# A selective-state kernel: TensorE's third state product moved behind exp(A) and the first two differences

## The reference

```python
proj = einsum('bsd,ed->bse', x, in_proj_w)            # gate, x/B/C, dt
hBC  = silu(causal_conv4(x/B/C) + conv_b)             # depthwise, 4 taps
L    = exp(segsum(dt * A))                            # decay inside a chunk
Y_diag = einsum('bzlhn,bzshn,bhzls,bzshp->bzlhp', C, B, L, x * dt)
states = einsum('bzlhn,bhzl,bzlhp->bzhpn', B, decay_states, x * dt)
prev   = states carried on from chunk to chunk with exp(A_last)
Y_off  = einsum('bzlhn,bzhpn,bhzl->bzlhp', C, prev, exp(A_cum))
y = (Y_diag + Y_off + x * D) * silu(gate)
out = einsum('bsi,oi->bso', rmsnorm_by_group(y) * norm_w, out_proj_w)
```

## Time and profile before

| what | value |
|---|---|
| median of 3 executions | 1913.36 us |
| profiled execution | 1919.0 us |
| its span | 1917.2 us |
| PE busy with matmuls | 1828.7 us, 95% |
| DVE busy | 1294.0 us, 67% |
| ACT busy | 1061.2 us, 55% |
| POOL busy | 938.7 us, 49% |
| mean granted TensorE clock | 0.983 of full speed |

### The profile page before, as it was taken

One profiled execution on the slowest core, in us unless ns is written; L12 is line 12 of the kernel. 1 busy time (PEld: TensorE's weight loads), 2 busy tenths in 40 slices (PEclk: granted clock), 3 DMA queues, 4 the chain that ended last, 5 costly groups with the idle time before them and its releaser, 6 DMA issues.

```text
span 1917.2 us, 31312 instructions
## 1 busy us (share of the span) xinstructions
PE 1828.7 (95%) x9752; PEld 1408.7 (73%) x9752; DVE 1294.0 (67%) x2094; ACT 1061.2 (55%) x1935; POOL 938.7 (49%) x717
## 2 busy tenths in 40 slices
PE   7889999999999999999999999999999999999966
PEld 6767778777777777777777777777777777777745
DVE  4856667666766667666676667666676666766688
ACT  5455555656546565555546565465665555565632
POOL 1225464555435465354645554354654545454564
PEclk9799999999999999999999999999999999999988
DMA  4412121121212121021211112121211212112121
GB/s 173 142 51 70 53 64 48 39 61 52 70 33 64 48 67 50 28 67 58 66 44 45 57 49 70 33 64 48 67 50 30 65 59 64 43 46 61 34 94 55
DMA packets 76393, 114.14 MB, mean 60 GB/s; under 512 B 21696, under 2 KB 27328, under 8 KB 75328
## 3 DMA queue, kind: packets, MB, share of 16 engines
q1 hardware_dynamic: 58656, 80.07, 14.2%
q10 hardware_dynamic: 17568, 31.99, 5.0%
HBM read 88.94 MB, written 23.07 MB: 58 GB/s over the span
## 4 chain that ended last, share of the span: by engine, by line
issue 45%; POOL 33%; PE 12%; DVE 4%; ACT 2%; DMA 1%; SPq 1%; POOLq 1%; ACTq 0%; DVEq 0%
POOL yt L1505 9%; POOL ssq L1500 6%; POOL wg_lo L1436 4%; POOL wo_lo L1436 4%; POOL prev L1486 3%; POOL yt L1508 3%; POOL wx_lo L1436 3%; PE bank L449 3%; PE bank L451 2%; PE bank L450 2%; PE bank L586 1%; PE bank L479 1%; PE bank L734 1%; PE bank L648 1%; PE bank L782 0%
## 5 line engine op out<-in xcount | busy, mean ns | idle before, releaser
L1505 POOL TENSOR_TENSOR yt<-yt,ea 128x384 f32<-128x384 f32 (+1 forms) x128 | 189.9, 1483 | 413.2 <-DVE ea L1352 413.2
L1136 DVE SCALAR_TENSOR_TENSOR xc<-bank,bpar,xc 128x511 f32<-128x511 f32 (+2 forms) x384 | 285.8, 744 | 63.4 <-ACT xc L848 58.9
L1322 DVE TENSOR_TENSOR lm<-lm,cbm 128x512 f32<-128x512 f32 x256 | 186.1, 768 | 164.5 <-ACT lm L993 164.5
L449 PE MATMUL bank<-h_hi,wg_hi 128*128 128x512 f32 x640 | 263.6, 412 | 16.7 <-ACT gate L949 13.9
L451 PE MATMUL bank<-h_hi,wg_lo 128*128 128x512 f32 x640 | 252.0, 394 | 0.0
L450 PE MATMUL bank<-h_lo,wg_hi 128*128 128x512 f32 x640 | 251.7, 393 | 0.0
L449 PE MATMUL bank<-wo_hi,g_hi 128*128 128x512 f32 x496 | 206.8, 417 | 6.1 <-POOL wo_lo L1436 6.1
L449 PE MATMUL bank<-h_hi,wx_hi 128*128 128x512 f32 x512 | 211.3, 413 | 1.1 <-DVE craw L1136 0.7
L1486 POOL TENSOR_TENSOR prev<-prev,dec 128x512 f32<-128x512 f32 x96 | 101.8, 1061 | 220.7 <-DVE prev L1271 132.3
L450 PE MATMUL bank<-h_lo,wx_hi 128*128 128x512 f32 x512 | 201.6, 394 | 0.0
L451 PE MATMUL bank<-h_hi,wx_lo 128*128 128x512 f32 x512 | 201.0, 393 | 0.0
(11 more groups left out here) (182 smaller groups left out, 3866.7 us busy)
## 6 DMA issues: line engine op xcount, KB each, us to landing
raw_w<-w_in_dram SPq DMA_DIRECT2D x145, 256.0 KB, 2.7
raw_w<-w_out_dram SPq DMA_DIRECT2D x64, 256.0 KB, 2.6
part_d<-part ACTq DMA_DIRECT2D x64, 256.0 KB, 2.1
part<-part_d ACTq DMA_DIRECT2D x58, 256.0 KB, 2.7
rt<-rows_d SPq DMA_DIRECT2D x256, 8.0 KB
acc<-x_dram SPq DMA_DIRECT2D x8, 256.0 KB, 6.6
acc<-w_mod_dram SPq DMA_DIRECT2D x2, 1024.0 KB, 6.4
lh<-neg_d SPq DMA_DIRECT2D x128, 8.0 KB
```

What stands on the lines that cost most here:

```text
L449: nc.tensor.matmul(out_ap, whi(k), hhi(k), start=(k == 0), stop=False)
L1136: stt(dst[:, at], ps[:, 0:HALF - 3 + k], w(k), dst[:, at], ALU.mult, ALU.add)\
L1322: tt(lm[:, h % 4, :], lm[:, h % 4, :], cbm[:, toks(hf)], ALU.mult).then_inc(v_m, 1)
L1505: tt(yt[:, j % 2, cols], yt[:, j % 2, cols], ea[:, j % 2, cols], ALU.add).then_inc(p_t3, 1)
```

## The change

On PE, at `z == 3` of every unit, `states(2)` is issued after `exp_a(0)`, `diff(0)` and `diff(1)` in place of ahead of them. No other engine's stream is touched, and nothing is added or removed.

```diff
                     if z == 3:
                         if not first and not end:
                             out_proj(u - 1, 2)
-                        states(2)
                         exp_a(0)
                         diff(0)
                         diff(1)
+                        states(2)
                     if not first and not (end and z > 0):
                         ...
                         out_proj(u - 1, z)
```

## The result

| | before | after |
|---|---|---|
| median | 1914.80 us (1911.96 to 1918.55, 20 runs) | 1919.51 us (1915.11 to 1923.28, 20 runs) |
| ratio to before | | 1.0022, 95% interval 1.0015 to 1.0029 |

What follows compares the result with a forecast made beforehand. PE's issue order and the gaps between its matmuls were taken to bound the kernel. -2.8 (PE's own cost) + 1.3 (first unit) + 0 = -1.5 us, from 1913.36 to 1911.9 us; range 1908.8 to 1916.8.

Steps and rivals of the forecast that it cites:

- PE's own cost: On PE, the new order takes 2.29 us in place of 2.41, kept in 23 units: 2.8 us saved.
- the first unit: Without projection cover, diff(1) waits for the fourth xw and states(3) starts 1.31 later: +1.3 us, bounds 0 and +1.3.
- whose first half is long enough to hide the late load: The second change of shape falls on the state product, which hides the late weight load: the 0.12 us goes.
- The step from the product to the output projection: The step without a row: 0.86 and 0.23 at its cheap end, taken; 0.95 and 0.35 at its dear end.
- the five steps: PE's new order: projection-exp(A) 0.32, exp(A)-difference 0.33, differences-product 0.55, product-projection 0.86, first projection matmul 0.23; sum 2.29 us.
- the 0.12: PE's saving per unit from the new order, 2.29 us for 2.41.
- The first rival: The saving isn't there, on PE; only the first unit's +1.3 counts: 1914.7 us, chance 0.17.
- Seven c = 3 units give their gain away: In c = 3 of groups 0 to 6, PE's 0.12 us is waited away at accumulate(3).
- An earlier ACT brings nothing: exp_a(0) comes 0.86 us earlier but hides in ACT's next wait: value 0.
- Nobody is late behind the product in the other `hf == 0` units: The product starts 0.97 us later, yet new_state(2) ends 1.78 us before states(3) is due.
- none of the four: Rivals: no saving (chance 0.17), dear new pair (0.09), states(3) waits in all hf == 0 units (0.04), ACT's gain reaches PE (0.09).
- The last unit: PE idles there anyway, absorbing two more changes of shape: value 0, bounds -0.3 and +1.3 us.

Runs made afterwards that it cites:

- e6: Against the kernel before: old order, exp_a(0), diff(0) and diff(1) on all 128 rows with weights zero outside the first 32; 1906.24 us, ratio 0.9965.
- e3: Against the kernel before: the new order in the last unit only; 1912.95 us, ratio 0.9992.
- e7: Against the kernel before: old order, but states(2) of the first unit also waits for the fourth xdt and xw; 1917.95 us, ratio 1.0022.
- e9: The changed kernel run once more, nothing altered; 1919.47 us.
- e1: Against the changed kernel: old order in the first unit only, new order in the 31 others; 1914.55 us, ratio 0.9998 to the kernel before.
- e4: Against the changed kernel: nine unread matmuls put into PE's idle time in the first unit; 1915.91 us, ratio 1.0002 to the kernel before.
- e10: e7 run once more, on another Trainium2 chip, nothing altered; 1921.03 us.
- e8: Against e7: six unread matmuls put ahead of the added wait in the first unit; 1914.88 us, ratio 1.0004 to the kernel before.

## Why the prediction was wrong

The forecast was -1.5 us and the change is +4.2. Two terms were mis-sized: the -2.8 for PE's own cost is 0, and the +1.3 for the first unit is 4.4.

- **PE's own cost: -2.8 us forecast, 0 measured.** The step "whose first half is long enough to hide the late load" failed. The state product behind the differences is recorded with 1.13 us in place of 1.02: the weight load of its second half lies open for 0.11. The step from the product to the output projection was right at its cheap end: from the product's start to the second projection matmul it is 1.19 us (1334.67 to 1335.86), which is the 0.86 and 0.23 of the forecast and this 0.11, to rounding. So of the five steps four came as read from rows, and the 0.12 was given back at the fifth. I had bounded only the step that had no row. The state product's own length stood in the sum at the value it has behind a full-array matmul, but it had changed its neighbour too. The first rival, "the saving isn't there", was right that the two orders cost the same, for the reason that it gives: the count of changes of shape, two in both. Its time, 1914.7 us, is not right either, for it takes the first unit at +1.3. The Trainium skill (TensorEngine Tiling (Array Packing), Key Properties) says that changing the tiling mode drains the engine. The trace agrees with a cost by the number of changes: 2.41 and 2.40 us with two, 2.02 with none (e6).
- **Seven c = 3 units give their gain away:** not tested by the change, since there was no gain. The waits there come to 6.1 us in 7, 1.7 less than before, but that is scatter: with the old order in these units they come to 7.4 in e3 and 5.8 in e7, with the new one to 6.9 in e9 and 5.1 in e1. e6 can't tell their gain from their scatter.
- **An earlier ACT brings nothing:** right, as far as e1's interval tells. Its wait fell by the 0.86 forecast (3.31 to 2.45), and e1 shows no gain.
- **Nobody is late behind the product in the other `hf == 0` units:** right. No wait at `states(3)`, which starts 4.91 us behind the last projection matmul of z = 2 (1333.46 to 1338.37) and did so in 4.93 before.
- **The first unit: the decisive miss.** The delay came nearly as worked out: `states(3)` 1.6 us later against the transposes, for 1.3 (DVE's end to PE's start took 0.14 us twice, not 0.04). The step that failed is "The bounds are 0 ... and +1.3": the wait was priced by its length alone. Before, PE's one wait there was 0.44 us; now there are 0.97 and 0.88 within 3 us, and behind them PE runs 6.7 us at 1.2 GHz. The end of the unit takes 4.4 us longer. Of these 1.4 are the delay (36.49 for 35.07 in e4, with full clock) and 3.0 the clock; in e7 and e10 it is 1.2 and 2.8. The medians agree: with the idle time filled, e4 and e8 lie 0.4 and 0.8 us above before, each give or take 2, where the change has 4.2. The page of before did show the kernel's sensitivity: its clock row has 9, 7, 9, 9 in the first four slices. I read only the stretch at full clock.
- **Rivals:** none of the four had the clock in it.
- **The last unit:** right at 0 (e3).

## What to carry to other kernels

Price a wait of PE by its length and by what the granted clock does behind it. Where PE has only just come out of idle time, as in a prologue or a first pass of a loop, 1.4 us more of waiting (0.97 and 0.88 for 0.44) cost this kernel 4.2 us, and matmuls that nobody reads, put into such a wait, gave back 3.8 (e4) and 3.4 (e8), each give or take 2 to 3. Before an order is moved, look for the pass that lacks the cover all others have; one of 32 decided here. Where matmuls of few rows stand between full ones, count the changes of shape: each pair costs 0.39 us here, behind an output projection as behind a state product, and zero-padded weights on all rows take it away.

## What the runs showed of the hardware

- A matmul of 16 rows costs as much as one of 128 with the same 512 columns (0.23 us from start to start behind one of its own shape), and the changes between the two cost more than the matmul itself (0.39 us a pair against 0.23).
- The same wait of 1.59 us was followed by full clock once and by half clock once (1.00 in e7 and 0.72 in e10 from 118 to 130 us), which made 2.8 us. One profile can miss the cause of a difference in medians.
- In the changed kernel's c = 2 units `mix(0)`, `mix(1)` on DVE and the decay on POOL now start together and both get longer: 2.15 us for 1.29 and 1.44 for 1.06. This is most of the growth of DVE's busy time (`mix` between 200 and 1800 us: 180.0 us for 167.3), and PE's waits for DVE did not grow in sum (7.4 us for 8.4).
